# Loading and splitting the next context earlier, and storing a batch's second weight sums in the batch after

## The chip, the cores and the metric

The kernel runs on one core of a Trainium2 chip. The metric is the time of one execution in microseconds on the device. TensorE (PE in the profile) multiplies, VectorE (DVE), ScalarE (ACT) and GpSimd (POOL) do elementwise work, and SyncE (SP) issues the transfers (DMAs) between the device's memory and the core's memory.

## The reference

Eight batches. Each has 112 rows of `x` (the latents) and 375 rows of a context, all 1024 wide.

```python
def attention(latents, context):           # latents = layernorm(x); 4 key/value heads, 32 query heads of 128
    hidden = concatenate([context, latents], axis=1)
    q = latents @ Wq                        # 1024 x 4096
    k, v = hidden @ Wk, hidden @ Wv         # 1024 x 512 each
    return softmax(q k^T / sqrt(128)) v @ Wo
x = x + attention(layernorm(x), ctx)
x = x + layernorm(relu(h @ up)**2 @ down + ((h @ fc1) @ expert * routing) @ fc2) * gamma + beta   # h = layernorm(x)
```

`routing` is the sum of each row's two largest gate logits.

## The kernel before

**Stages.** The kernel goes through a context stage, a latent stage, a query stage, attention with the output product, and the feed-forward part. Every product is made of three matmuls on operands split in two: `hi` is the value rounded to TensorE's fp32r format (ACT makes it), `lo` is what is left (a subtraction on DVE or POOL).

**The context stage.** It makes keys and values of the contexts. A batch is seven units, each with its own PSUM bank: four of keys (K0 to K3, one for each key/value head) and three of values (V0 to V2, 125 rows each). A unit is 24 matmuls. Its result is split by ACT (`ctx_unit_hi`) and DVE (`ctx_unit_lo`, helper `lo`, L1024). K0 to K3 go through two staging buffers `KST`, in turn, and SP stores each on its own. So ACT may split K2 only when the store of K0 has landed, K3 after that of K1, and the next batch's K0 and K1 after those of K2 and K3. The three V units share one staging buffer and one store (L474).

The context itself arrives in one buffer, `CRAW`. ACT splits its `hi` (L793, after K1 of the batch that runs), POOL its `lo` (`ctx_lo`, L668), into one of two halves of `act_region`. TensorE starts batch b when the `lo` of its context is there (`s_clo`).

**The weight sums.** The query stage multiplies with a scheme that needs fewer products (seven blocks in place of eight), and for that wants four sums of blocks of each of 16 pairs of query-weight slabs. They are made during the context stage: SP loads a pair (two slabs of 512 KB, `load_pair`, L452) into `slab_raw`, POOL makes four sums in place (`weight_sums`, L679), and SP stores them (`store_sums`, L456). There is one such buffer, so the next pair is loaded when the store of the last has landed (`s_sst`). Two pairs are made in each batch, 2b and 2b + 1.

**Order.** Every engine runs its instructions in the order in which they are written, SP's too: a transfer behind a wait is issued when that wait is over. SP's order of a batch is that of `store_ctx(b)`, with `next_ctx(b)` ahead of it from batch 1 on. POOL's order of a batch is the sums of one pair, `ctx_lo`, the sums of the other:

```python
                for j in range(2):
                    weight_sums(4 * i + 2 * j + 2)
                    ctx_lo(2 * i + j + 2, j)
                    weight_sums(4 * i + 2 * j + 3)
```

**The last batch.** In batch 7 TensorE also transposes the normalised rows of `x`, two groups for each batch (`ln_group`, L1428). A group waits until ACT (L867) and DVE (L1127) have taken the one before it out of its bank, and ACT takes group u after unit u - 1. Then come the latent keys (`kl`) and values (`vl`), and in the latent stage SP loads the seven blocks of the first pair for the query stage (L483), once all sums are stored (`s_sst` at 16 times 16).

Of the kernel before, what the change touches and what calls it, by code (L numbers as in the profile page):

```python
# [12 lines left out]
B, SQ, HID = 8, 112, 1024  # L13
# [20 lines left out]
PAIRS = NH // 2  # L34
# [37 lines left out]
N_CTX = NKV + 3  # L72
# [41 lines left out]
C_LAT = N_CTX * B  # L114
# [23 lines left out]
def xattn_ffn(nc, x, ctxT, slabs, wkv, gate, gamma, beta, out):  # L138
    with ExitStack() as top:
# [3 lines left out]
        def sem(name):  # L143
            return top.enter_context(nc.semaphore(name))
# [28 lines left out]
        def part(t, at, n):  # L173
            return t[:, at:at + n]

        def f32(ap):
            return ap.bitcast(F32)
# [61 lines left out]
        CRAW = part(FB, 0, NK * SC).rearrange("p (k n) -> p k n", k=NK)  # L239
# [57 lines left out]
        s_sst = sem("weight_sums_stored")  # L297
# [14 lines left out]
        s_ctx = sem("ctx_loaded")  # L312
# [18 lines left out]
        s_ev = sem("group_taken")  # L331
# [7 lines left out]
        s_clo = sem("ctx_lo")  # L339
# [76 lines left out]
        def _(sp):  # L416
# [33 lines left out]
            def load_pair(j):  # L450
                for s in range(2):
                    sp.dma_start(RAWS[s], slabs[T_Q + 2 * j + s]).then_inc(s_rawq, 16)  # L452

            def store_sums(j):
                sp.wait_ge(s_sum, 4 * (j + 1))
                sp.dma_start(s_d[j], RAW[:, :]).then_inc(s_sst, 16)  # L456

            def store_ctx(b, first=False):
                for u in range(NKV):
                    sp.wait_ge(s_ev, N_CTX * b + u + 1)  # L460
                    sp.dma_start(kc_d[u, b], f32(KST[u % 2][:, :, 0:SC])).then_inc(s_kst[u % 2], 16)
                    if u == 0:
                        if not first:
                            sp.wait_ge(s_sst, 32 * b)
                        load_pair(2 * b)
                    if u == 2:
                        store_sums(2 * b)
                    if u == 3:
                        sp.wait_ge(s_sst, 32 * b + 16)
                        load_pair(2 * b + 1)  # L470
                sp.wait_ge(s_ev, N_CTX * b + N_CTX - 1)
                store_sums(2 * b + 1)
                sp.wait_ge(s_ev, N_CTX * b + N_CTX)
                sp.dma_start(v_d[:, b, :, 0:6 * D].rearrange("h p c -> p h c"),  # L474
                             f32(part(RC, 0, 6 * NKV * D)).rearrange("p (h c) -> p h c", h=NKV)).then_inc(s_vst, 16)

            def load_block(j, n):
                name = BLOCKS[n]
                if name[0] == "S":
                    block = s_d[j, :, SUMS[name] * 512:(SUMS[name] + 1) * 512]  # L480
                else:
                    block = slabs[T_Q + 2 * j + int(name[1]) - 1, :, (int(name[2]) - 1) * 512:int(name[2]) * 512]
                sp.dma_start(WRAW[n], block).then_inc(s_wr[n], 16)  # L483

            def next_blocks(j):
                for n in range(N_Q):
                    sp.wait_ge(s_blo, N_Q * j + n + 1)
                    load_block(j + 1, n)

            def next_ctx(b):  # L490
                sp.wait_ge(s_clo, b)
                sp.dma_start(CRAW, ctxT[b + 1]).then_inc(s_ctx, 16)

            store_ctx(0, True)
            with sp.Fori(1, B - 1) as b:
                next_ctx(b)
                store_ctx(b)
            store_ctx(B - 1)
            n = C_LAT
            for g in SEG1:  # L500
                if g[0] == "kl":
                    _, m, h = g
                    sp.wait_ge(s_ev, n + 1)
                    sp.dma_start(kl_d[m, :, :, h * HALF:(h + 1) * HALF], f32(KST[n % 2][:, :, 0:HALF])).then_inc(s_kst[n % 2], 16)
                    n += 1
                    if n == C_LAT + 2:
                        sp.wait_ge(s_sst, 16 * PAIRS)
                        sp.wait_ge(s_clo, B - 1)
                        for i in range(N_Q):
                            load_block(0, i)  # L510
                if g[0] == "vl":
                    b = g[1]
                    if n == N_UNITS - 1:
                        next_blocks(0)
                    sp.wait_ge(s_ev, n + 1)
                    sp.dma_start(v_d[:, b, 0:SQ, 6 * D:8 * D].rearrange("h p c -> p h c"),
                                 f32(part(YR, 4 * ROWS + b % 2 * HID, HID))[0:SQ, :].rearrange("p (h c) -> p h c", h=NKV)
                                 ).then_inc(s_vlst[b % 2], 16)
                    n += 1
# [121 lines left out]
        def _(pool):  # L641
# [24 lines left out]
            def ctx_lo(b, j):  # L666
                pool.wait_ge(s_chi, b)
                pool.tensor_tensor(HT[j][:, 1, :, 0:SC], CRAW, f32(HT[j][:, 0, :, 0:SC]), ALU.subtract).then_inc(s_clo, 1)  # L668


            def weight_sums(j):

                pool.wait_ge(s_rawq, 32 * (j + 1))
                W11, W12, W21, W22 = [part(RAW, i * 512, 512) for i in range(4)]
                for n, (out, a, b, op) in enumerate([(W22, W21, W22, ALU.add), (W21, W11, W21, ALU.subtract),
                                                     (W11, W22, W11, ALU.subtract), (W12, W12, W11, ALU.subtract)]):
                    if n:
                        pool.wait_ge(s_sum, 4 * j + n)
                    pool.tensor_tensor(out, a, b, op).then_inc(s_sum, 1)  # L679
# [3 lines left out]
            weight_sums(1)  # L683
            with pool.Fori(0, B // 2 - 1) as i:
                for j in range(2):
                    weight_sums(4 * i + 2 * j + 2)
                    ctx_lo(2 * i + j + 2, j)
                    weight_sums(4 * i + 2 * j + 3)
            weight_sums(PAIRS - 2)
            weight_sums(PAIRS - 1)  # L690
# [671 lines left out]
        def _(pe):  # L1362
# [110 lines left out]
            for j, g in enumerate(SEG1):  # L1473
                second = SEG1[j - 1][1] if j >= 2 and SEG1[j - 1][0] == SEG1[j - 2][0] == "ln" else None
                if g[0] == "ln":
                    if SEG1[j - 1][0] != "ln":
                        ln_group(g[1])
                    continue
                if g[0] == "ctx":
                    ctx_product(B - 1, g[1], 1, second)  # L1480
                elif g[0] == "kl":
                    _, m, h = g
                    pe.wait_ge(s_ev, n - N_CTX + 1)
                    pe.wait_ge(s_lnlo, 8 * h + 8)
                    for k in range(NK):
                        if k == 4 and second is not None:
                            ln_group(second)
                        last = k_step(unit_bank(n)[:, 0:HALF], lambda l, k: XT[h][:, l, k, :], m, k)
                    last.then_inc(s_mm, 1)
                else:  # L1490
                    b = g[1]
                    pe.wait_ge(s_ev, n - N_CTX + 1)
                    cols = slice(b % 4 * SQ, (b % 4 + 1) * SQ)
                    for k in range(NK):
                        last = v_step(unit_bank(n)[0:SQ, :], lambda l, k: XT[b // 4][:, l, k, cols], k)
                    last.then_inc(s_mm, 1)
                n += 1
# [252 lines left out]
```

## Time and profile before

| | |
|---|---|
| median of 3 runs | 1878.79 us (1877.6 to 1879.47) |
| the profiled execution | 1877.65 us |
| its span, first to last instruction | 1875.8 us |
| mean granted TensorE clock | 0.982 of full speed |
| PE busy | 1800.2 us, 96% of the span |
| POOL busy | 746.4 us, 40% |
| DVE, ACT busy | 738.5 us and 647.2 us, 39% and 35% |

The profile is of one execution, taken by the hardware. What lies outside the span (1.85 us) is starting and ending. The context stage takes the first 340 us or so, the latent stage lasts to about 430 us. Engine times in a view are from the start of the span.

### The profile page before, as it was taken

The numbers are of one execution on the slowest core, as the hardware profiler recorded it, in microseconds if no ns is written. First come the engines' busy times: TensorE is split into PE (matmuls) and PEld (weight loads), VectorE is DVE, ScalarE is ACT, GpSimd is POOL, SyncE is SP. The second block draws the span as 40 slices with busy tenths as digits, with TensorE's granted clock in tenths as the row PEclk, the third lists the DMA queues.
The fourth block names the chain that finished last, engine by engine and source line by source line (L and its number), as shares of the span: only waits on it lengthen the run. The fifth ranks groups of instructions, "written<-read, shape, count | busy, mean of one in ns | idle before, by whom it ended". The sixth has DMA issues, their size and how long they took to land.

```text
span 1875.8 us, 27532 instructions
## 1 busy us (share of the span) xinstructions
PE 1800.2 (96%) x9254; PEld 1622.8 (87%) x9254; DVE 738.5 (39%) x1239; ACT 647.2 (35%) x1256; POOL 746.4 (40%) x539
## 2 busy tenths in 40 slices
PE   8679998999999999999999999999999999999996
PEld 7578887979999988989998999899888989988886
DVE  3331001364443347732771376147434432212216
ACT  3111111223433347721771276147423213212321
POOL 3244334134555536542543245225456322222242
PEclk9889999999999999999999999999999999999998
DMA  8565675426667655431342144125234231111134
GB/s 281 189 231 201 241 247 212 177 86 210 203 217 258 228 176 176 144 105 64 127 160 78 57 160 146 64 85 163 92 124 180 79 101 56 56 56 45 56 102 168
DMA packets 127409, 271.95 MB, mean 145 GB/s; under 512 B 17024, under 2 KB 75392, under 8 KB 124416
## 3 DMA queue, kind: packets, MB, share of 16 engines
q1 hardware_dynamic: 127360, 271.29, 43.4%
q8 instruction: 32, 0.52, 0.1%
q14 instruction: 17, 0.14, 0.0%
HBM read 185.57 MB, written 85.69 MB: 145 GB/s over the span
## 4 chain that ended last, share of the span: by engine, by line
PE 55%; issue 27%; POOL 12%; DMA 3%; DVE 1%; ACT 1%; POOLq 0%; SPq 0%; ACTq 0%; DVEq 0%
PE bank L1369 18%; PE bank L1371 18%; PE bank L1370 18%; POOL tile_region L713 6%; POOL slab_raw L679 3%; POOL slab_split L654 2%; POOL act_region L668 2%; PE bank L1562 1%; DMA slab_raw<-in_slabs 1%; DMA k_ctx_scratch<-small_region 1%; PE bank L1399 0%; DMA q_scratch<-y_region 0%; ACT slab_split L755 0%; PE bank L1428 0%; DMA weight_sums_scratch<-slab_raw 0%
## 5 line engine op out<-in xcount | busy, mean ns | idle before, releaser
L654 POOL TENSOR_TENSOR slab_split<-slab_raw,slab_split 128x1024 fp32r<-128x1024 f32 x94 | 225.0, 2394 | 463.6 <-ACT slab_split L755 463.6
L1369 PE MATMUL bank<-act_region,slab_split 128*128 128x512 f32 (+2 forms) x992 | 361.2, 364 | 1.7 <-DVE mid_region L1024 1.2
L1371 PE MATMUL bank<-act_region,slab_split 128*128 128x512 f32 (+2 forms) x992 | 361.2, 364 | 0.0
L1370 PE MATMUL bank<-act_region,slab_split 128*128 128x512 f32 (+2 forms) x992 | 360.8, 364 | 0.0
L713 POOL TENSOR_TENSOR tile_region<-tile_region,small 128x487 f32<-128x487 f32 x224 | 216.1, 1001 | 208.2 <-DVE small L1139 208.2
L755 ACT ACTIVATE slab_split<-slab_raw 128x1024 fp32r<-128x1024 f32 x94 | 99.4, 1057 | 378.7 <-PE bank L1371 378.5
L1369 PEld LDWEIGHTS bank<-act_region,slab_split 128*128 128x128 f32 x992 | 186.6, 188 | 22.7 <-issue 2.3
L1176 DVE TENSOR_TENSOR y_region<-y_region,bank 128x512 f32 (+2 forms) x96 | 59.6, 621 | 365.6 <-PE bank L1371 365.6
L1370 PEld LDWEIGHTS bank<-act_region,slab_split 128*128 128x128 f32 x992 | 186.4, 188 | 19.4
L1371 PEld LDWEIGHTS bank<-act_region,slab_split 128*128 128x128 f32 x992 | 186.4, 188 | 18.8
L1369 PE MATMUL bank<-mid_region 128*128 128x488 f32 (+2 forms) x480 | 198.9, 414 | 2.1 <-DMA mid_region<-k_latents_scratch 1.6
L1371 PE MATMUL bank<-mid_region 128*128 128x488 f32 (+2 forms) x480 | 180.5, 376 | 0.0
L1370 PE MATMUL bank<-mid_region 128*128 128x488 f32 (+2 forms) x480 | 180.4, 376 | 0.0
L1369 PE MATMUL bank<-mid_region,slab_split 128*128 128x512 f32 (+2 forms) x448 | 163.3, 365 | 1.7 <-DVE mid_region L1024 1.7
L1143 DVE TENSOR_REDUCE small<-bank 128x1 f32<-128x487 f32 x224 | 146.0, 653 | 45.4 <-PE bank L1371 45.4
L1371 PE MATMUL bank<-mid_region,slab_split 128*128 128x512 f32 (+2 forms) x448 | 163.3, 364 | 0.0
L1370 PE MATMUL bank<-mid_region,slab_split 128*128 128x512 f32 (+2 forms) x448 | 163.1, 364 | 0.0
L889 ACT ACTIVATE tile_region<-bank,small 128x487 f32<-128x487 f32 x224 | 153.5, 685 | 27.2 <-DVE small L1143 27.2
L897 ACT ACTIVATE mid_region<-bank 125x512 fp32r<-125x512 f32 x224 | 136.7, 611 | 74.2 <-PE bank L1562 74.2
L1369 PE MATMUL bank<-act_region,mid_region 128*128 128x376 f32 (+1 forms) x320 | 116.5, 364 | 44.8 <-POOL act_region L668 37.2
L679 POOL TENSOR_TENSOR slab_raw<-slab_raw 128x512 f32<-128x512 f32 x64 | 83.5, 1304 | 185.5 <-DMA slab_raw<-in_slabs 181.8
L1163 DVE TENSOR_TENSOR mid_region<-bank,mid_region 125x512 fp32r<-125x512 f32 x224 | 152.5, 682 | 10.1 <-ACT mid_region L897 10.1
(147 smaller groups left out, 3064.3 us busy)
## 6 DMA issues: line engine op xcount, KB each, us to landing
slab_raw<-in_slabs SPq DMA_DIRECT2D x126, 512.0 KB, 3.5
q_scratch<-y_region SPq DMA_DIRECT2D x16, 1792.0 KB, 8.1
mid_region<-q_scratch SPq DMA_DIRECT2D x32, 896.0 KB, 5.6
weight_sums_scratch<-slab_raw SPq DMA_DIRECT2D x16, 1024.0 KB, 4.0
v_scratch<-slab_split SPq DMA_DIRECT2D x8, 1536.0 KB, 8.5
slab_raw<-weight_sums_scratch SPq DMA_DIRECT2D x48, 256.0 KB, 4.4
mid_region<-v_scratch SPq DMA_DIRECT2D x32, 384.0 KB, 3.1
k_ctx_scratch<-small_region SPq DMA_DIRECT2D x32, 375.0 KB, 6.0
```

The lines of the kernel that those rows point to most:

```text
L654: pool.tensor_tensor(WS[s][1], RAWS[s], f32(WS[s][0]), ALU.subtract).then_inc(s_wlo, 1)
L679: pool.tensor_tensor(out, a, b, op).then_inc(s_sum, 1)
L713: pool.tensor_tensor(PR[i][:, 0:KEYS], PR[i][:, 0:KEYS], rrow[:, i:i + 1].broadcast_to([P, KEYS]), ALU.mult).then_inc(s_pn, 1)
L755: act.activation(WS[s][0], RAWS[s], ACT.Copy).then_inc(s_whi, 1)
L889: act.activation(PR[i][:, 0:KEYS], SB[RING[i]][:, 0:KEYS], ACT.Exp, bias=negmax[:, i:i + 1], accum_out=rowsum[:, i:i + 1]).then_inc(s_exp, 1)
L897: act.activation(PT[0][0:KT, :, i * P:(i + 1) * P], TB[RING[i]][0:KT, :].rearrange("p (t n) -> p t n", t=4), ACT.Copy).then_inc(s_pth, 1)
L1143: dve.reduce_max(negmax[:, i:i + 1], SB[RING[i]][:, 0:KEYS], AX.X, negate=True).then_inc(s_max, 1)
L1163: dve.tensor_tensor(PT[1][0:KT, :, cols], TB[RING[i]][0:KT, :].rearrange("p (t n) -> p t n", t=4), f32(PT[0][0:KT, :, cols]), ALU.subtract ...
L1176: dve.tensor_tensor(Y[:, m, cols], Y[:, m, cols], gb(c_static)[:, 0:PARTS[h][1] - PARTS[h][0]], ALU.add).then_inc(s_ev, 1)
L1369: pe.matmul(out_ap, w[0], a[0], start=first, stop=False)
L1370: pe.matmul(out_ap, w[0], a[1], start=False, stop=False)
L1371: return pe.matmul(out_ap, w[1], a[0], start=False, stop=last)
```

## The change

SP, in `store_ctx(b)`:
- the pair 2b is loaded after the store of K1, not after that of K0;
- the sums of the pair 2b - 1 are stored in batch b, between K0 and K1; before, they were stored at the end of batch b - 1;
- the context b + 2 is loaded after K3 of batch b, once the `lo` of context b + 1 is made; before, it was loaded ahead of the first store of batch b + 1 (`next_ctx`, which is gone), behind the store of the V units of batch b;
- the sums of the pair 2b are stored and the pair 2b + 1 loaded behind that, and the V units last;
- the sums of the last pair are stored in the latent stage, behind the first latent-key store.

POOL: `ctx_lo(b + 1)` comes ahead of the sums of pair 2b, where it stood between the two pairs of batch b. No instruction and no transfer is added or taken away. ACT, DVE and TensorE keep their order.

```diff
-            def store_ctx(b, first=False):
+            def store_ctx(b, first=False, last=False):
+
                 for u in range(NKV):
                     sp.wait_ge(s_ev, N_CTX * b + u + 1)
                     sp.dma_start(kc_d[u, b], f32(KST[u % 2][:, :, 0:SC])).then_inc(s_kst[u % 2], 16)
-                    if u == 0:
+                    if u == 0 and not first:
+                        store_sums(2 * b - 1)
+                    if u == 1:
                         if not first:
                             sp.wait_ge(s_sst, 32 * b)
                         load_pair(2 * b)
-                    if u == 2:
-                        store_sums(2 * b)
-                    if u == 3:
-                        sp.wait_ge(s_sst, 32 * b + 16)
-                        load_pair(2 * b + 1)
-                sp.wait_ge(s_ev, N_CTX * b + N_CTX - 1)
-                store_sums(2 * b + 1)
+                if not last:
+                    sp.wait_ge(s_clo, b + 1)
+                    sp.dma_start(CRAW, ctxT[b + 2]).then_inc(s_ctx, 16)
+                store_sums(2 * b)
+                sp.wait_ge(s_sst, 32 * b + 16)
+                load_pair(2 * b + 1)
                 sp.wait_ge(s_ev, N_CTX * b + N_CTX)
...
-            def next_ctx(b):
-                sp.wait_ge(s_clo, b)
-                sp.dma_start(CRAW, ctxT[b + 1]).then_inc(s_ctx, 16)
-
             store_ctx(0, True)
-            with sp.Fori(1, B - 1) as b:
-                next_ctx(b)
+            with sp.Fori(1, B - 2) as b:
                 store_ctx(b)
-            store_ctx(B - 1)
+            for b in range(B - 2, B):
+                store_ctx(b, False, True)
...
                     n += 1
+                    if n == C_LAT + 1:
+                        store_sums(PAIRS - 1)
                     if n == C_LAT + 2:
                         sp.wait_ge(s_sst, 16 * PAIRS)
...
                 for j in range(2):
+                    ctx_lo(2 * i + j + 2, j)
                     weight_sums(4 * i + 2 * j + 2)
-                    ctx_lo(2 * i + j + 2, j)
                     weight_sums(4 * i + 2 * j + 3)
```

## Rows read from the trace of the kernel before

**Rows 1.** The page: span.

```profile
span 1875.8 us, 27532 instructions
```

**Rows 2.** Waits of TensorE, 20 to 400 us: waited for, us in total, times, longest.

```profile
PE bank L1369 <- POOL act_region L668: 37.2, 5, 22.7
PE bank L1428 <- issue: 3.7, 1, 3.7
PE bank L1428 <- DVE act_region L1127: 3.3, 1, 3.3
```

**Rows 3.** Timeline of TensorE: start us, duration us, instruction, [idle before it].

```profile
42.60 0.34 PE L1369 MATMUL bank<-act_region,mid_region 128*128 128x376 f32 x1
...
98.83 0.68 PE L1369 MATMUL bank<-act_region,mid_region 128*128 128x376 f32 x1 [22.72 <-POOL act_region L668]
...
138.75 0.68 PE L1369 MATMUL bank<-act_region,mid_region 128*128 128x376 f32 x1 [4.38 <-POOL act_region L668]
...
294.68 0.98 PE L1428 MATMUL bank<-ident,y_region 112*128 112x112 f32 x4 [3.71 <-issue]
...
317.64 0.57 PE L1428 MATMUL bank<-ident,y_region 112*128 112x112 f32 x4 [3.27 <-DVE act_region L1127]
```

**Rows 4.** Windows: stretch, length, each engine's busy time, then PEclk, DMA share, GB/s.

```profile
42.60:76.10 33.50, 33.50 (x169) 29.75 (x167) 3.78 (x7) 2.00 (x5) 9.63 (x8) 1.00 0.54 204
...
294.60:300.00 5.40, 5.32 (x25) 5.35 (x26) 0.62 (x1) 0.54 (x1) 0.61 (x1) 0.71 0.57 185
...
317.60:324.00 6.40, 6.36 (x23) 5.12 (x24) 1.08 (x2) 0.92 (x2) 5.13 (x4) 0.73 0.31 103
```

**Rows 5.** Timeline of POOL: start, time of the group, instruction, [idle before].

```profile
58.19 5.40 POOL L679 TENSOR_TENSOR slab_raw<-slab_raw 128x512 f32<-128x512 f32 x4 [10.88 <-DMA slab_raw<-in_slabs]
86.79 5.95 POOL L679 TENSOR_TENSOR slab_raw<-slab_raw 128x512 f32<-128x512 f32 x4 [23.21 <-DMA slab_raw<-in_slabs]
92.70 5.99 POOL L668 TENSOR_TENSOR act_region<-tile_region,act_region 128x3000 fp32r<-128x3000 f32 x1
...
183.06 5.40 POOL L679 TENSOR_TENSOR slab_raw<-slab_raw 128x512 f32<-128x512 f32 x4 [4.91 <-DMA slab_raw<-in_slabs]
```

**Rows 6.** Timeline of SP: start and time of issuing, transfer.

```profile
53.41 0.81 SPq L452 DMA_DIRECT2D slab_raw<-in_slabs  x2
63.66 0.34 SPq L456 DMA_DIRECT2D weight_sums_scratch<-slab_raw  x1
64.04 0.43 SPq L474 DMA_DIRECT2D v_scratch<-slab_split  x1
64.82 0.73 SPq L492 DMA_DIRECT2D tile_region<-in_ctxT  x1
...
172.33 0.37 SPq L456 DMA_DIRECT2D weight_sums_scratch<-slab_raw  x1
...
176.45 0.90 SPq L452 DMA_DIRECT2D slab_raw<-in_slabs  x2
```

**Rows 7.** Transfers issued at 306.2, 64.8, 93.5 and 172.3 us: KB each, us to landing.

```profile
k_ctx_scratch<-small_region SPq DMA_DIRECT2D x1, 375.0 KB, 9.7
...
tile_region<-in_ctxT SPq DMA_DIRECT2D x1, 1500.0 KB, 11.2
...
k_ctx_scratch<-small_region SPq DMA_DIRECT2D x1, 375.0 KB, 5.6
...
weight_sums_scratch<-slab_raw SPq DMA_DIRECT2D x1, 1024.0 KB, 3.9
```

**Rows 8.** Timeline of ACT: start, duration, instruction, [idle before].

```profile
76.06 2.70 ACT L793 ACTIVATE act_region<-tile_region 128x3000 fp32r<-128x3000 f32 x1 [30.44 <-DMA tile_region<-in_ctxT]
...
315.90 0.48 ACT L765 ACTIVATE small_region<-bank 128x375 fp32r<-128x375 f32 x1 [9.56 <-DMA k_ctx_scratch<-small_region]
...
393.01 0.62 ACT L844 ACTIVATE slab_split<-slab_raw 128x512 fp32r<-128x512 f32 x1
```

**Rows 9.** Timeline of DVE, 93 to 100 us.

```profile
93.89 5.35 DVE L1042 TENSOR_SCALAR y_region<-y_region,small 112x1024 f32<-112x1024 f32 x1
```

## The prediction

> **What bounds the kernel now.** I read the page first: the span is 1875.8 us [rows 1] and TensorE is busy in nearly all of it, so a gain can only come from where TensorE stands still, or runs at the lower of its two clocks. I then asked for TensorE's waits in the first 400 us, since the change touches nothing later. There are seven [rows 2]: five for POOL's `ctx_lo`, 37.2 us together, one of 3.7 us ahead of batch 7 whose releaser is not named ("issue"), but which is the same wait (the first group of batch 7 stands behind the same semaphore), and one of 3.3 us inside batch 7, for DVE. Everything before the stage's first wait and all that follows batch 7 shows no wait that the change could touch.
>
> The timeline gives the places [rows 3]. Batch 1 starts at 42.60 and ends at 98.83 - 22.72 = 76.11 us: 33.51 us, and the reader should see that this batch ran at a granted clock of 1.00 [rows 4]. That is the undisturbed price of a batch. Batch 2 starts at 98.83, batch 7 at 294.68, so five batches take 195.85 us, 39.17 each. Of the 5.66 us above 33.51, some 3.6 are the wait (18.1 us in five), and 2.0 are the half clock that follows: a matmul lasts 0.68 us at the first start after a wait, 0.34 where TensorE was not interrupted [rows 3]. The windows say it of batch 7: a granted clock of 0.71 over its first 5.4 us, and of 0.73 over the 6.4 us after the 3.27 us wait inside it [rows 4] (a mix of the levels 1.2 and 2.4 GHz).
>
> Why does TensorE wait? On POOL and SP one sees two causes. First, batch 2: SP issues context 2 at 64.82, because `next_ctx` is queued behind the store of the sums of pair 1, 63.66, which had to wait for POOL, 58.19 + 5.40 = 63.6 [rows 5, 6]. It lands at 76.0 [rows 7]; ACT splits it [rows 8], and then POOL does the sums of pair 2 first, 86.79 to 92.7, and `ctx_lo` until 98.7 [rows 5]. Second, the later batches: context, pair, sums and store make a ring, each waiting for the one before it, that is 39.17 us long against TensorE's 33.51.
>
> **The change, part by part.**
>
> *The ring of the sums by itself.* Every pair goes through load, four sums and store, with one buffer. From a store's issue, 172.33, over the next pair's load, 176.45, to POOL's start, 183.06, and its end 5.40 later, 188.46 [rows 5, 6] is 16.1 us, and with the 0.2 us to the next store 16.3. No context load disturbs that half. Two pairs are 32.6 us, 0.9 less than TensorE's batch. This is the number on which the forecast rests: in the new order nothing else stands in this ring, as `ctx_lo` (6.0 us) falls into the 10.7 us in which POOL waits for store and load.
>
> *Context 2, the first batch.* The context goes out after K3 of batch 0, before the store of the sums of pair 0. The pair 1 load, at 53.41, and its sums, ending at 63.6, stay where they are [rows 5, 6]; the context is loaded beside them and ACT's split (2.7 us [rows 8]) is over long before 63.6. `ctx_lo(2)` then runs 63.6 to 69.6. TensorE wants it at 76.11: no wait, 6.5 us to spare, and 22.7 us are gone. Should the context's 1500 KB hold up the sums' store, the spare time takes it: the worst bound is its whole 11.2 us [rows 7], which would leave a wait of 4.7 us.
>
> *The later batches.* Call E the end of the sums of pair 2b - 1. `ctx_lo(b + 1)` ends at E + 6, and the next E is 32.6 later. With E = 63.6 for batch 1, `ctx_lo(7)` ends at 69.6 + 5 x 32.6 = 232.6, against 76.11 + 5 x 33.51 = 243.7 when TensorE wants it. The spare time even grows. So batch 7 starts at 243.7 in place of 294.68: 51.0 us. (The same by its terms: 37.2 + 3.7 of waits, 10.1 of half clock in five batches.)
>
> *What is queued behind the new waits.* The store of the sums of 2b - 1 now stands ahead of the store of K1. S is the start of the batch on TensorE; of its 33.51 us a key unit takes 376 / (4 x 376 + 3 x 512) by its columns, 4.1 us, a value unit 5.6. So K1 is ready at S + 9.4, splits included, while E is at S + 21 in batch 1 and at S + 16 in batch 7: K1's store goes late by 6 to 12 us. It lands 5.6 us later, as K3's did behind such a store [rows 7]; K3's split waits for that, and with it the V splits, at E + 7.4. TensorE wants K3's bank again at the next batch's fourth unit, 33.5 + 12.4 = S + 45.9: cover of 17 us and more. The context load waits for K3 and goes out at E + 8; its split is needed 24 us later. V's store moves behind the pair's load, and its buffer is wanted a batch later. All of it costs nothing; if the cover were gone, each us of E would be one of TensorE's.
>
> *Inside batch 7.* TensorE stood 3.27 us since K0's store, issued at 306.18, took 9.7 us [rows 7] and ACT's split of K2 and the transposed rows were behind it, at 315.90 [rows 8]. That store was issued late, as SP sat in the wait for the sums of pair 13 ahead of it. Now K0 goes first and the sums second. Pair 13 goes out at E - 11.7 = S + 3.9; it, V and K0 are 2935 KB, 8.9 us at the rate under rival A, so K0 lands by S + 13, when K2 is done (three units of 4.1 and three groups of 0.5 us). K1's store goes at E = S + 16, K3's split starts at S + 22, and the transposed group behind it is wanted at S + 24.6. I take this wait as gone, with the clock behind both it and the start: 5.4 x 0.29 = 1.6 and 6.4 x 0.27 = 1.7 us [rows 4]. The bounds are 0 and 3.3 + 1.7 = 5.0 for the wait.
>
> *The end.* The sums of the last pair are over at 63.6 + 7 x 32.6 = 291.8 and stored by 296. The blocks of the query stage, loaded behind them, are first read at 393.01 [rows 8], less the gain: 335. Some 39 us of cover, so nothing.
>
> *POOL and DVE.* In batch 1 DVE normalises the rows of `x`; these now fall beside other POOL work. One such instruction lasted 5.35 us, ending 0.5 us after the `ctx_lo` beside which it ran [rows 5, 9], and the sums at 86.79 took 5.95 where others took 5.40 [rows 5]. I count up to 0.6 us twice on E of batch 1, inside its 6.5 us. The Trainium skill ("SBUF — State Buffer", section "Who interferes with whom") says that DVE in its two-port mode and GpSimd take one shared pair of ports by an exclusive lock, so that the second waits for the whole instruction of the first. The trace agrees with its 5.35 us. By that rule DVE would be held up to 6 us by `ctx_lo(2)`, and POOL under 1 us at a time; neither reaches TensorE.
>
> Sum: 51.0 + 1.6 + 3.3 + 1.7 = 57.6 us. The profiled execution becomes 1877.65 - 57.6 = 1820.0; its median lies 1.14 us above it, so 1821.2 us.
>
> **Rivals.**
>
> *A. The context load holds up the ring.* It now stands ahead of the store of the sums of pair 2b in the same queue. A K store behind one of 1536 KB took 9.7 us, against 5.6 behind one of 1024 KB [rows 7]. If the sums' store takes 5.8 us more (9.7 for 3.9), a round takes 38.4 us: `ctx_lo(7)` ends at 69.6 + 192 = 261.6, the gain up to batch 7 is 33.1, the rest is not to be had, and the time is 1845.7. Against it: pair, two K stores and context are 3274 KB from E + 4.3 on. At the 328 KB per us of the three transfers issued from 63.66 to 64.82 (4060 KB, the last landed at 76.0) [rows 6, 7], they are through at E + 14.3, before the sums of 2b end at E + 16. The point from which it bites is a round of 33.5 + 6.5 / 5 = 34.8 us, and at 36 us the time is 1834. The Trainium skill ("DMA: Bandwidth & Descriptors", section "Queues, rings and completion order") has each of the 16 engines take the descriptors of one issuing engine in ring order. By it, a context issued a few us before the sums would be ahead of them with all it has left. The 9.7 us agree. Chance 0.15 for A in all, most of it near 1834.
>
> *B. The wait in batch 7 stays*, or one of like size takes its place (K3 behind the late K1, which has 3 us to spare only): 1821.2 + 5.0 = 1826.2. Chance 0.22.
>
> *C. Slower.* SP's one queue closes a longer ring: K1 behind the sums, K3 behind K1, the context behind K3, ACT's split behind the context, POOL's sums behind that. Every step is a wait for a landing. It is slower than before from a round of (294.68 - 69.6) / 5 = 45.0 us on, 12.4 above my sum; at 46 it gives 1884. By the rows this ring has 20 us of slack. Chance 0.02.
>
> *D. The gain is eaten later*, by the blocks of the query stage coming late. That would need over 39 us on the last sums; a chance of 0.01, near the time before.
>
> **The numbers.** All waits gone 0.60, B 0.22, A 0.15, C 0.02, D 0.01. The range runs from 1817 (a clock that recovers a little better, the execution's own scatter) to 1836, which takes in B and the near part of A; about 0.1 is left above, in A, C and D, and a little below. Some 0.2% (3.8 us) is what a measurement of this kernel can tell from no change. Faster 0.97, same 0.01, slower 0.02.
>
> **What would show it.** TensorE without a wait for L668, batches 33.5 us long, batch 7 starting near 244; POOL doing L668 directly behind four L679 and a gap of 5 us before the next; 32.6 us from one E to the next (A if it is 36 or more); context loads landing 12 us before ACT's L793; no wait at L1428 (else B). The prediction is wrong if the ring of the sums is longer than 34.8 us with a context in it, as I have only seen the half without one.

## The result and the profile after

The changed kernel takes 1827.07 us (median of 4 runs, 1824.39 to 1833.43), against 1878.19 us before (4 runs, 1877.41 to 1879.47). The ratio is 0.9732, with a 95% interval of 0.9705 to 0.9759: 51.1 us less, where 57.6 were forecast. The profiled execution takes 1825.77 us, its span is 1824.0 us and its mean granted clock 0.994, against 0.982.

TensorE's waits from 20 to 400 us, which were seven [rows 2], are one:

```profile
PE bank L1428 <- DVE act_region L1127: 5.6, 1, 5.6
```

The timeline of TensorE at the starts of batches 1, 2, 5 and 7 and at that wait (to be read beside [rows 3]). No start of a batch carries a bracket, the mark of idle time, any more:

```profile
43.06 0.34 PE L1369 MATMUL bank<-act_region,mid_region 128*128 128x376 f32 x1
...
76.41 0.33 PE L1369 MATMUL bank<-act_region,mid_region 128*128 128x376 f32 x1
...
176.45 0.33 PE L1369 MATMUL bank<-act_region,mid_region 128*128 128x376 f32 x1
...
243.14 0.55 PE L1428 MATMUL bank<-ident,y_region 112*128 112x112 f32 x4
...
267.00 0.98 PE L1428 MATMUL bank<-ident,y_region 112*128 112x112 f32 x4 [5.59 <-DVE act_region L1127]
```

The windows say the same by stage (stretch, length, busy times, then granted clock, DMA share, GB/s). The clock is 1.00 in batches 1 to 6, and the transfers carry 269 GB/s, against 204 in batch 1 before [rows 4]; the last row holds the wait in batch 7 and the half clock behind it:

```profile
109.40:142.90 33.50, 33.50 (x171) 30.00 (x170) 4.21 (x9) 6.42 (x9) 16.35 (x9) 1.00 0.80 269
...
210.00:243.50 33.50, 33.50 (x173) 30.01 (x171) 4.12 (x7) 6.33 (x9) 16.36 (x9) 1.00 0.83 268
...
260.00:271.00 11.00, 5.41 (x21) 4.43 (x20) 1.08 (x2) 0.92 (x2) 5.03 (x4) 0.71 0.75 276
```

The timeline of POOL shows the new order, `ctx_lo` (L668) directly behind the second pair's four sums (L679), and then a gap in which the next pair is stored and loaded (to be read beside [rows 5]):

```profile
44.72 5.40 POOL L679 TENSOR_TENSOR slab_raw<-slab_raw 128x512 f32<-128x512 f32 x4 [11.28 <-DMA slab_raw<-in_slabs]
63.23 5.41 POOL L679 TENSOR_TENSOR slab_raw<-slab_raw 128x512 f32<-128x512 f32 x4 [13.11 <-DMA slab_raw<-in_slabs]
68.59 6.09 POOL L668 TENSOR_TENSOR act_region<-tile_region,act_region 128x3000 fp32r<-128x3000 f32 x1
79.10 5.73 POOL L679 TENSOR_TENSOR slab_raw<-slab_raw 128x512 f32<-128x512 f32 x4 [4.42 <-DMA slab_raw<-in_slabs]
...
234.12 6.09 POOL L668 TENSOR_TENSOR act_region<-tile_region,act_region 128x3000 fp32r<-128x3000 f32 x1
...
259.96 5.30 POOL L679 TENSOR_TENSOR slab_raw<-slab_raw 128x512 f32<-128x512 f32 x4 [10.15 <-DMA slab_raw<-in_slabs]
```

`ctx_lo(2)` ends at 68.59 + 6.09 = 74.7 us; TensorE starts batch 2 at 76.41. It is on time by 1.7 us. From the first to the last of the six (context 2 to 7) it is (234.12 - 68.59) / 5 = 33.1 us a round, against TensorE's (243.14 - 43.06) / 6 = 33.35 us a batch. So both run at nearly one pace.

Where the 51.9 us of the two profiled executions come from: the first operation of POOL in the query stage is a good mark for the end of all that the change touches. It goes from 393.7 to 343.5 us, 50.2 us. (The view of that line, first the kernel before, then the one after.)

```profile
L695 POOL TENSOR_TENSOR slab_split<-slab_raw,slab_split x64: 1283/1292/3082, 393.7 to 674.2; 128x512 fp32r<-128x512 f32 x64
```

```profile
L695 POOL TENSOR_TENSOR slab_split<-slab_raw,slab_split x64: 1284/1292/3079, 343.5 to 623.9; 128x512 fp32r<-128x512 f32 x64
```

The query stage is as long as before (280.5 and 280.4 us). The rest lies behind it, in the attention stage, whose work is the same in both: from POOL's first to its last normalising operation it is 632.9 us before, 631.0 after, and 633.3 in one of the kernels below.

### The profile page after: what moved, and what is told of

The parts are those of the page before. It is cut to its first block, busy times and chain, and to the rows that moved or that the text cites. A ratio compares the mean times of both kernels' runs of the same rounds, so it can differ in the third digit from the quotient of the medians.

```text
span 1824.0 us, 27488 instructions
## 1 busy us (share of the span) xinstructions
PE 1788.4 (98%) x9254; PEld 1611.7 (88%) x9254; DVE 737.5 (40%) x1239; ACT 647.7 (36%) x1256; POOL 746.6 (41%) x539
## 4 chain that ended last, share of the span: by engine, by line
PE 55%; issue 26%; POOL 14%; DMA 2%; DVE 1%; ACT 1%; POOLq 1%; SPq 0%; ACTq 0%; DVEq 0%
PE bank L1369 18%; PE bank L1371 17%; PE bank L1370 17%; POOL tile_region L713 7%; POOL slab_raw L679 3%; POOL act_region L668 2%; POOL slab_split L654 2%; PE bank L1562 1%; DMA slab_raw<-in_slabs 1%; DMA weight_sums_scratch<-slab_raw 1%; PE bank L1399 1%; DMA k_ctx_scratch<-small_region 1%; ACT slab_split L755 0%; PE bank L1428 0%; DVE small L1031 0%
## 5 line engine op out<-in xcount | busy, mean ns | idle before, releaser
L1562 PEld LDWEIGHTS bank<-ident,tile_region 128*125 128x125 f32 x896 | 132.5, 188 | 16.7 <-issue 2.3
L679 POOL TENSOR_TENSOR slab_raw<-slab_raw 128x512 f32<-128x512 f32 x64 | 82.8, 1294 | 142.6 <-DMA slab_raw<-in_slabs 138.8
```

Of the source, the lines that this page charges most:

```text
L1562: last = pe.transpose(TB[RING[i]][0:KT, t * P:(t + 1) * P], PR[i][:, t * KT:(t + 1) * KT], ident[:, :])
```

## The experiments

Times of single executions are called so. Beside these runs the kernel before took 1875.3 to 1875.7 us, and 1878.8 us beside the last of them. "The mark" is POOL's first operation of the query stage, as above; it leaves out all later scatter.

**The changed kernel again.**

> The changed kernel once more, to see whether its spread (1824.4 to 1833.4 us) comes back and to have a profile of another execution. If the spread comes from TensorE having little to spare (in the profiled execution the lo of context 2 was ready 1.2 us before TensorE wanted it), another profile shows the same seven batches of 33.5 us or one with a wait for L668, and the wait at L1428 in batch 7 varies between 4 and 8 us. If the spread comes from elsewhere, the context stage is alike to 0.5 us.

A median of 1826.25 us (5 runs, 1824.34 to 1827.64), ratio 0.9738 (0.9725 to 0.9752). Its profile has the same seven batches without a wait for L668, the wait at L1428 at 4.9 us, and the mark at 342.4. The stage is alike to 1.1 us, of which 0.7 are that wait. The execution of 1833 us did not come back; what made it so long stays open.

**POOL's order alone.**

```diff
                 for j in range(2):
+                    ctx_lo(2 * i + j + 2, j)
                     weight_sums(4 * i + 2 * j + 2)
-                    ctx_lo(2 * i + j + 2, j)
```

> Only POOL's order is changed (ctx_lo ahead of both pairs' sums), SP's order is that of before. If TensorE waited because POOL did sums first, five waits shrink by the 5.4 us of the sums: nearly all are gone, and the time is 1840 or less. My theory: the sums stand in a ring (load, sums, store, load, sums, store, context load) that is longer than TensorE's batch; with SP's old order, ctx_lo ahead of the sums makes the ring longer by its 6 us, since pair 2b and the context land together. Then batch 3 starts near 131, and each batch after takes 43 to 45 us: batch 7 starts at 303 to 310, and the time is 1885 to 1895, slower than before.

One execution of 1899.28 us (the kernel before on the same chip: 1875.32). Slower by 24 us, and by the mechanism that was expected: TensorE's batches 4 to 7 start at 172.62, 216.32, 259.65 and 303.26, 43.5 us apart. The two operations of POOL that follow a context load:

```profile
166.49 6.00 POOL L668 TENSOR_TENSOR act_region<-tile_region,act_region 128x3000 fp32r<-128x3000 f32 x1 [16.03 <-ACT act_region L793]
172.45 5.32 POOL L679 TENSOR_TENSOR slab_raw<-slab_raw 128x512 f32<-128x512 f32 x4
```

`ctx_lo` now comes first, and the sums of the pair, which had landed with the context, come 6 us later; the rest of the ring follows. TensorE's `lo` comes earlier in a round that is longer. What I had not put into the sum is batch 7, where the same lateness reaches K2's split and TensorE waits 14.5 us at L1428 (the waits of TensorE, 20 to 400 us):

```profile
PE bank L1369 <- POOL act_region L668: 29.3, 4, 8.1
PE bank L1428 <- DVE act_region L1127: 14.5, 1, 14.5
PE bank L1369 <- DVE slab_split L1024: 10.4, 1, 10.4
PE bank L1428 <- issue: 7.2, 1, 7.2
```

The 10.4 us stand ahead of batch 3, where `ctx_lo` (123.23 + 6.00) and a split of V on DVE (127.36 + 1.89) end within 0.02 us of each other; the 7.2 us stand ahead of batch 7. So each of the six batches from 2 to 7 starts with a wait, 46.9 us together, against 40.9 before. The mark is at 413.7, 20.0 us later than before.

**SP's order alone.** The changed kernel with POOL's loop of before (sums, `ctx_lo`, sums).

```diff
                 for j in range(2):
-                    ctx_lo(2 * i + j + 2, j)
                     weight_sums(4 * i + 2 * j + 2)
+                    ctx_lo(2 * i + j + 2, j)
```

> Only SP's order is changed, POOL's is that of before (sums, ctx_lo, sums). If the earlier context load is what brings the gain, the time is near 1830. My theory: SP waits for ctx_lo(b + 1) before it stores the sums of pair 2b, and POOL does ctx_lo only after those sums, so 6 us of ctx_lo and part of the context's load stand in the ring: 33.1 + 6.1 = 39.2 us at least, 43 with a store held up by the context. Batch 2 starts near 91, batch 7 between 287 and 306: a time of 1867 to 1890.

One execution of 1883.32 us, 8 us slower than before, with the mark at 400.5, 6.8 us later. The batches start 43.1 us apart (133.10 to 305.51 in four). SP's timeline shows both costs that make the round longer: it gets to the context load and the sums' store only when `ctx_lo` is done (126.98 + 5.99 = 132.97), and the store is then held up by the context in front of it, 9.0 us to landing where 3.9 do by itself [rows 7]:

```profile
133.14 0.34 SPq L471 DMA_DIRECT2D tile_region<-in_ctxT  x1
133.77 0.36 SPq L456 DMA_DIRECT2D weight_sums_scratch<-slab_raw  x1
142.96 0.97 SPq L452 DMA_DIRECT2D slab_raw<-in_slabs  x2
```

So neither half of the change pays by itself: +24 and +8 us, and -49 to -51 together. POOL's order takes `ctx_lo` out of the way of TensorE, SP's order moves the context load to where the ring has room for both.

**K0 and K1 of batch 7 early.** To find out about the 5.6 us that are left. `store_key(c, u)` waits for key unit u of batch c and stores it, as the loop did; the comments are added here.

```diff
                 for u in range(NKV):
+                    if u == 0 and key0_done:          # b == 7
+                        store_key(b, 1)
+                    if not (u < 2 and key0_done):
+                        store_key(b, u)
...
                 store_sums(2 * b)
+                if key0_next:                         # b == 6
+                    store_key(b + 1, 0)
                 sp.wait_ge(s_sst, 32 * b + 16)
                 load_pair(2 * b + 1)
```

> The changed kernel, and for batch 7 alone K0's store goes ahead of the load of pair 13 and the V store of batch 6, and K1's ahead of the store of the sums of pair 13. If the wait at L1428 (5.6 us, and 1.7 to 3 us of half clock behind it) is there because K2's split waits for K0's store, which SP issued 6.5 us after it was ready, the wait is gone, the profile shows batch 7 without any, and the time falls by 7 us (0.4%) against the changed kernel. If the landing itself were slow whatever stands ahead, the wait stays within 2 us.

A median of 1820.42 us (5 runs, 1817.75 to 1827.35), ratio to the kernel before 0.9714 (0.9695 to 0.9733), 5.8 us under the changed kernel on the same chip, where 7 were expected; the interval still touches the changed kernel's (0.9725 to 0.9752). No wait of TensorE from 20 to 400 us is over 0.5 us. This is the version to keep; run again beside two others below:

> K0 and K1 of batch 7 early, once more on the chip of the two others, for the comparison: a median of 1818 to 1822 us, 0.3% under the changed kernel, and a profile in which TensorE has no wait of over 0.5 us in the first 400 us.

1819.79 us (5 runs, 1818.16 to 1819.95), ratio 0.9701 (0.9688 to 0.9715), now clear of the changed kernel's interval. The mark is at 336.2 (335.9 in the first set), 6.2 to 7.6 us ahead of the changed kernel's two (342.4 and 343.5), and the waits are:

```profile
PE bank L1436 <- DVE act_region L1135: 0.5, 1, 0.5
PE bank L1377 <- ACT tile_region L935: 0.2, 1, 0.2
```

(L1436 is the `ln_group` line of this kernel, L1377 the first matmul of a product.)

**K0 alone early.** As above, with K1 left behind the store of the sums of pair 13.

> The changed kernel with K0 of batch 7 alone stored early (K1 stays behind the sums of pair 13). If K2's wait for K0 is the whole of batch 7's trouble, this is as fast as with K0 and K1 early, a span near 1817. My theory of the queue says that the wait moves: K1's store goes out at 265.7, K3's split at 271.5, and TensorE, which wants the group behind it at 243.1 + 24.6 = 267.7, waits 4 to 5 us at L1428: a span near 1822.

One execution of 1828.78 us, span 1827.0 (near 1822 expected), the mark at 344.3: nothing gained. K2's split runs at 256.72, when TensorE is done with it, and the wait has moved to K3's, which stands behind K1's store. It is longer than expected, 7.1 us, in part since TensorE gets there 0.6 us sooner (267.1) and K3's split comes 1 us later (272.45, 271.5 expected). The timeline of ACT:

```profile
256.72 0.48 ACT L771 ACTIVATE small_region<-bank 128x375 fp32r<-128x375 f32 x1 [3.61 <-PE bank L1377]
257.10 0.54 ACT L873 ACTIVATE act_region<-bank 128x448 fp32r<-128x448 f32 x1
272.45 0.48 ACT L771 ACTIVATE small_region<-bank 128x375 fp32r<-128x375 f32 x1 [14.81 <-DMA k_ctx_scratch<-small_region]
```

**Pair 0 loaded first.**

```diff
-                    if u == 1:
-                        if not first:
-                            sp.wait_ge(s_sst, 32 * b)
+                    if u == 1 and not first:
+                        sp.wait_ge(s_sst, 32 * b)
                         load_pair(2 * b)
...
+            load_pair(0)
             store_ctx(0, True)
```

> The changed kernel with pair 0 loaded ahead of K0 of batch 0, where nothing holds it back. The sums of pair 1 ended at 68.6 where 63.6 was forecast. If that comes from pair 0 landing late (sums from 44.7 in place of 41.9), POOL's first sums start 2 to 3 us earlier and those of pair 1 end near 66; if it comes from the context load in front of the sums' store, they still end at 68 or more. TensorE has no wait there, so the span stays within 1 us of 1823, but for batch 7's wait, which follows the end of the sums and may shrink by 2 us.

One execution of 1826.54 us, span 1824.7. POOL's first sums do start earlier (42.16 against 44.72), but those of pair 1 end at 70.5, not at 66: later than in the changed kernel. The sums' store was issued at 47.60, 1.3 us behind the context load at 46.30, and took 11.4 us. TensorE waits 0.5 us ahead of batch 2, where no wait was expected, and the span is 0.7 us above what was expected. So an earlier pair 0 alone wins nothing: what it gains, its store loses to the context in front of it, and the earlier the sums are ready, the more of the context they have ahead of them.

**The context behind the second pair.**

```diff
-                if not last:
-                    sp.wait_ge(s_clo, b + 1)
-                    sp.dma_start(CRAW, ctxT[b + 2]).then_inc(s_ctx, 16)
                 store_sums(2 * b)
                 sp.wait_ge(s_sst, 32 * b + 16)
                 load_pair(2 * b + 1)
+                if not last:
+                    sp.wait_ge(s_clo, b + 1)
+                    sp.dma_start(CRAW, ctxT[b + 2]).then_inc(s_ctx, 16)
```

> The changed kernel with the context load moved behind the sums' store and the load of pair 2b + 1 (still ahead of the V store). If the context in front of the sums' store lengthens the ring (rival A), the half with the store falls from 17 to 16.3 us, a round from 33.1 to 32.5 us, and the sums of pair 1 end near 64. In its place the context comes 12 us later: in batch b + 1 ACT waits for it after K1, and ctx_lo is bound by it and no more by the sums. I expect the context to land at E + 30, its split at E + 33, ctx_lo at E + 39 against E + 38.6 without: a tie, TensorE with waits of 0 to 2 us and a span of 1822 to 1832.

One execution of 1834.09 us, span 1832.3, the mark at 351.6. Of the first half of the expectation one part holds: the store of the sums of pair 0 lands in 3.9 us, and those of pair 1 end at 59.12 + 5.39 = 64.5. The round does not fall to 32.5 us: from context 3 on `ctx_lo` starts (241.10 - 107.42) / 4 = 33.4 us apart. The context now stands ahead of the store of the other pair, 2b + 1, which takes 7.1 to 8.7 us in batches 2 to 6. Its cost has moved from one store to the other. The landings of the same store (KB, us) in the changed kernel, in this one, and with pair 0 first:

```profile
weight_sums_scratch<-slab_raw SPq DMA_DIRECT2D x1, 1024.0 KB, 6.8
```

```profile
weight_sums_scratch<-slab_raw SPq DMA_DIRECT2D x1, 1024.0 KB, 3.9
```

```profile
weight_sums_scratch<-slab_raw SPq DMA_DIRECT2D x1, 1024.0 KB, 11.4
```

The second half was a little too kind (the span is 0.3 us above its range): `ctx_lo` now waits for the context (POOL's gaps of 2.2 to 4.1 us ahead of it, as 98.0 + 5.4 to 107.4), TensorE has two waits of 3.8 us together for it, and batch 7's wait is 8.4 us. The place chosen by the change is the better one, though it costs the ring something.

**The ring longer.** One more POOL addition in the sums of each pair, its result unused.

```diff
                     if n:
                         pool.wait_ge(s_sum, 4 * j + n)
+                    if n == 1:
+                        pool.tensor_tensor(part(FB, 3500, 512), W11, W12, ALU.add)
```

> The changed kernel with one more POOL addition of 512 columns (1.35 us) in each pair's sums, its result unused. POOL is idle half of the time, so if TensorE alone set the pace this would cost nothing: a span near 1823. If the ring of the sums is what TensorE has 0.4 us of spare in a batch against, the round grows from 33.1 to 35.8 us: ctx_lo(2) ends at 77.4 (a wait of 1.5 us), each later batch takes 35.8, batch 7 starts near 256.5 in place of 243.1, and the span is 1835 to 1842.

One execution of 1836.16 us, span 1834.3, the mark at 353.9: 10.4 us later than in the changed kernel, on an engine that is idle for half of this stage. `ctx_lo` starts (243.25 - 70.05) / 5 = 34.6 us apart, not 35.8: of 2.5 us added to a round (the sums of a pair take 6.66 us in place of 5.40) only 1.5 arrive. Sums that are ready later find less of the context in front of their store, which gives back a part: in batches 1 to 5 the store behind the context lands in 3.9 us four times and in 5.7 once, where the changed kernel has 4.3 to 5.9. TensorE pays 4.0 us in two waits for L668, batch 7's wait is 9.6 us in place of 5.6.

**`ctx_lo` twice.** The subtraction is made twice from context 2 on, with a wait between, the second result replacing the first.

```diff
+                if not isinstance(b, int):
+                    pool.tensor_tensor(HT[j][:, 1, :, 0:SC], CRAW, f32(HT[j][:, 0, :, 0:SC]), ALU.subtract).then_inc(s_dup, 1)
+                    pool.wait_ge(s_dup, b - 1)
                 pool.tensor_tensor(HT[j][:, 1, :, 0:SC], CRAW, f32(HT[j][:, 0, :, 0:SC]), ALU.subtract).then_inc(s_clo, 1)
```

> The changed kernel with ctx_lo done twice (6.1 us more) from context 2 on, the first result overwritten. POOL waits 11 us in that half of the ring, so the ring itself hardly grows; only TensorE's spare time is spent. By my theory ctx_lo(2) ends at 80.8 us, TensorE waits 5 us ahead of batch 2 and 1 to 2 us more further on, batch 7 starts at 249 to 253 in place of 243.1, and the span is 1830 to 1836. If TensorE had the 6.5 us to spare that the prediction gave it, the wait ahead of batch 2 would be 0 and the span 1823 to 1825.

One execution of 1838.07 us, span 1836.3, the mark at 348.6. TensorE starts batch 2 at 80.54 after a wait of 3.5 us (5 expected), has one of 0.5 us later, and one of 4.5 us in batch 7. The mark is 5.1 us later than in the changed kernel; the span's other 7 us lie behind it, 4.7 of them in a query stage of 285.1 us, see the next. TensorE has some 3 us to spare ahead of batch 2 in this execution (its last matmul before was issued at 76.67, the first `ctx_lo` ended at 67.90 + 6.08 = 74.0), not 6.5.

**Context 2 late.** K0 and K1 of batch 7 early, and context 2 alone loaded behind the second pair.

```diff
-                if not last:
+                if not last and not first:
                     sp.wait_ge(s_clo, b + 1)
...
                 load_pair(2 * b + 1)
+                if first:
+                    sp.wait_ge(s_clo, b + 1)
+                    sp.dma_start(CRAW, ctxT[b + 2]).then_inc(s_ctx, 16)
```

> K0 and K1 of batch 7 early, and context 2 alone loaded behind the sums' store and pair 1. The store then lands in 3.9 us in place of 6.8, the sums of pair 1 end at 64.5 and ctx_lo(2) near 73 in place of 74.7. No wait of TensorE is left to remove, so the time is that of the kernel with K0 and K1 early within 2 us, if its spread (1817.8 to 1827.4) comes from elsewhere; if the spread comes from a wait ahead of batch 2 in some executions, the slowest of five runs is under 1822.

1824.78 us (5 runs, 1821.49 to 1827.95), ratio 0.9726 (0.9712 to 0.9739): 5 us over the version without this edit, beside which it ran, where 2 at most were expected. It has waits of 0.5 and 1.7 us in the stage, and its mark is at 338.7, 2.5 us later. SP's timeline shows why: the sums of pair 1 are ready at 59.39 + 5.41 = 64.8, but their store goes out at 68.67, behind that of K0, whose split stands behind the context's on ACT (63.88 to 66.6). That is no earlier than the 68.82 of the changed kernel, and the load of pair 2 follows at 76.33, against 72.92 there. What the profiled execution has on top is in the query stage, which is the same program:

> The kernel with context 2 late (and K0 and K1 of batch 7 early) once more. Its profile had the query stage 4.7 us longer than the others (285.3 in place of 280.6 us from POOL's first to its last operation there), with TensorE's matmuls 205 ns apart in place of 201 at a granted clock of 1.00 and no wait. If that belongs to the execution (a rhythm into which TensorE falls), this profile shows 280.6 or 285.3 as it comes, and the times spread over 1818 to 1828; if it belongs to the program, it is 285.3 again and no time is under 1821.

A median of 1823.12 us (4 runs, 1821.27 to 1825.31), and the query stage is 280.4 us long this time. The mark is at 338.7 again. The windows of the two executions of this one program, 400 to 450 us, first the longer, then the shorter:

```profile
400.00:450.00 50.00, 50.00 (x244) 45.41 (x243) 19.61 (x32) 19.50 (x36) 25.84 (x20) 1.00 0.66 212
```

```profile
400.00:450.00 50.00, 50.00 (x249) 46.33 (x248) 20.04 (x33) 19.12 (x36) 27.12 (x21) 1.00 0.67 220
```

244 and 249 matmuls in 50 us, 205 and 201 ns apart, at a granted clock of 1.00 and a busy share of 1 in both. So this does not belong to the program. The two ran on different chips, but on the chip of the longer one the version without this edit took 280.6 us with 249 matmuls in this window, and `ctx_lo` twice 285.1 us with 244; so it is not the chip alone either. The 2.5 us at the mark do belong to the edit: both profiles have them. No time was under 1821 in either set.

## Why the prediction was nearly right, and where it was not

**Two causes of the waits: shown.** Both were needed. With POOL's order alone the ring stays and is even 43.5 us long; with SP's alone it is 43.1. Each was one execution, but these lengths repeat over three and four batches.

**Up to batch 7: right, to 0.6 us.** Batch 7 was to start at 243.7 and starts at 243.14. Batches of 33.4 us at full clock, no wait for L668, as the prediction said they would be seen. The margin was far smaller than it said: `ctx_lo(7)` ends at 240.2, 2.9 us before TensorE wants it, where 11.1 were forecast (232.6 against 243.7).

**The ring of 32.6 us: a little short.** It is 33.1 with a context in it. The half with the context has its store land in 4.3 to 5.9 us in batches 1 to 5, where 3.9 were counted. The prediction had the context through at E + 14.3, before those sums are ready; in batch 1 it went out at 78.23 and landed 9.4 us later, at E + 19.0, and the sums were ready at E + 16.2. From context 4 on ACT even waits 0.5 to 1.7 us for it, where it was to lie there for 12 us; TensorE does not see that wait, as `ctx_lo` comes 10 us and more after the split. This is rival A in small: its mechanism is real, its size in the steady batches is 0.5 us a round, and it stays under the 34.8 us at which it would have decided. By its 5.8 us a store it was put too high for this order; with SP's order alone, where the context is issued 0.6 us ahead of the store, the store takes 9.0 us. The Trainium skill ("DMA: Bandwidth & Descriptors", section "Queues, rings and completion order") has the descriptors of one issuing engine taken in ring order on each of the 16 engines. The 3.9, 6.8, 9.0 and 11.4 us of one and the same store, with 1500 KB of context issued never, 5.9, 0.6 and 1.3 us before it, agree in that the load in front holds up the store, though the third and fourth stand in another order than their leads, so something else counts as well, and no run here shows what.

**Context 2: the term that was mis-sized.** "The pair 1 load, at 53.41, and its sums, ending at 63.6, stay where they are" did not hold: the load went out at 56.91 and the sums ended at 68.64, 5.0 us late. Of these, 2.8 us are there when the sums of pair 0 begin (44.72, against 41.90 before), 0.7 come with their store (6.8 us to landing against 6.1 before, where no context stood in front; why it took 6.1 there stays open) and 1.5 with the load of pair 1 (6.3 us to POOL's start against 4.8). The context's share is what comes back without it: with the context behind the pair, pair 0's sums begin as late (44.83) and pair 1's end at 64.5, 4.1 us earlier. The prediction had named the context in front of that store as a bound and let the spare time take it, which it did (1.7 us of 6.5 were left), but went on with 63.6 in the steps behind.

**Inside batch 7: the step that failed.** It said that pair 13 goes out at S + 3.9 and that K0 lands by S + 13. With the late sums carried on, pair 13 went out at 253.75, S + 10.6, and K0 behind it and V at 255.08; it landed 10.2 us later, S + 22. Pair 13, V and K0 took 11.5 us from the first issue, where the prediction counted 8.9. SP's timeline:

```profile
249.84 0.35 SPq L456 DMA_DIRECT2D weight_sums_scratch<-slab_raw  x1
253.75 0.81 SPq L452 DMA_DIRECT2D slab_raw<-in_slabs  x2
254.60 0.43 SPq L476 DMA_DIRECT2D v_scratch<-slab_split  x1
255.08 0.54 SPq L462 DMA_DIRECT2D k_ctx_scratch<-small_region  x1
265.29 0.34 SPq L456 DMA_DIRECT2D weight_sums_scratch<-slab_raw  x1
```

and ACT, at K2's split:

```profile
265.25 0.48 ACT L765 ACTIVATE small_region<-bank 128x375 fp32r<-128x375 f32 x1 [11.88 <-DMA k_ctx_scratch<-small_region]
```

K0 had been ready near 249; SP stood before the sums of pair 12 and then before their landing. TensorE waited 5.59 us where 0 were forecast and 3.27 were there before, plus the half clock. That is rival B, at 1826.2 us, and the measured 1827.07 is near its time. The nearness is in part luck: by the mark the gain is 50.2 and 51.3 us in the two profiles, 7.4 and 6.3 short of 57.6, where B counts 5.0; in the first profile the attention stage, which the change does not touch, gives 1.9 us back. The forecast of 1821.2 is what the kernel with K0 and K1 early reaches (1820.42 and 1819.79), where the wait is taken away; its mark of 336.2 is 393.7 - 57.5.

**"It lands 5.6 us later and all of it costs nothing": right for batches 1 to 6.** K1's stores there land in 5.4 to 6.5 us. ACT waits 148.8 us in total for stores of keys, where it waited 41.9 us, and TensorE does not see it, since its banks are free for a batch. In batch 7 the transposed groups stand behind the same splits, and the cover is gone; K0 early alone showed that K3's split, behind K1, had none either: E was S + 22, not S + 16.

**C and D** did not come. The last sums are stored by 300, the query stage needs them at 343. **POOL and DVE:** one normalising instruction beside `ctx_lo(2)` took 5.44 us where others take 0.81, as forecast, and the sums of pair 2 took 5.73 and 6.28 us in two executions where others take 5.40; neither reached TensorE.

## What to carry to other kernels

Follow a moved wait into the place where the stage ends: there other work can stand behind the same splits, so that the cover for a late store is gone, and a queue in written order holds up a transfer that has long been ready. When several engines and a queue go round in a ring, time the ring by itself and against the engine that should set the pace; an edit that takes one station out of that engine's way while making the ring longer is a loss, and two edits that each lose can gain together. A load in front of a store in one queue can be a cost of the store (up to 7.5 us here), and the spare time it eats must be carried into every later step of the sum.

## What the runs showed of the hardware

- One program's query stage took 280.4 or 285.3 us in two executions, with no wait and a granted clock of 1.00 in both, the matmuls 201 or 205 ns apart; a third execution, of another version, took 285.1 us. It can be a share of the spread of 2 to 10 us within the sets of the changed kernels; what sets it stays open.
- A 1024 KB store of the same form took 3.9 to 4.3 us to land in most places with no context in front of it in SP's queue (6.1 at its first in the kernel before), and 6.8, 9.0 and 11.4 us with 1500 KB of context issued 5.9, 0.6 and 1.3 us before it.
